# Two channel tiles per scan with start states from TensorE in layer 0, and separate banks and later steps for the token chain in layers 1 and 2

## The reference, cut to what matters

```python
# layer 0: selective scan over the 2304 pixels of an image, 768 inner channels, 16 states
xz = xs @ in_proj_w.T                 # 384 -> 1536: xin and gate z
xin = silu(causal_conv4(xin) + conv_b)
dt, Bm, Cm = split(xin @ x_proj_w.T);  dt = softplus(dt @ dt_proj_w.T + dt_proj_b)
h = exp(dt * A) * h + dt * Bm * xin   # per pixel, channel and state
y = einsum(h, Cm) + xin * D;           out = layernorm((y * silu(z)) @ out_proj_w.T)
# layer 1: 1x1 product, a filter on 8x8 blocks in the Fourier domain, 3x3 depthwise, gelu gate, 1x1 product
# layer 2: 11x11 depthwise convolution whose kernels have 4 free points
# layer 3: two of four experts per pixel, each 384 -> 384 -> 384
```

## Time and profile before

| | us |
|---|---|
| three runs | 6280.98 median, 6262.24 to 6282.42 |
| profiled execution | 6270.08, of which span 6268.3 |
| TensorE busy | 5086.3 (81%) |
| DVE busy | 4781.1 (76%) |
| ACT busy | 2805.0 (45%) |
| POOL busy | 2379.9 (38%) |
| mean granted TensorE clock | 0.927 |

### The profile page before, as it was taken

The page is one execution under the profiler, slowest core; times in us unless marked ns, Lnnn a source line. Parts: engine busy times, 40 slices in busy tenths (PEclk is TensorE's granted clock), DMA queues, the critical chain, the costliest instruction groups (busy, mean ns, idle before and its releaser), DMA issues.

```text
span 6268.3 us, 78225 instructions
## 1 busy us (share of the span) xinstructions
PE 5086.3 (81%) x28644; PEld 3933.0 (63%) x28644; DVE 4781.1 (76%) x6523; ACT 2805.0 (45%) x4858; POOL 2379.9 (38%) x2894
## 2 busy tenths in 40 slices
PE   5787888887888887888888876677777787999999
PEld 3565656655656655666655554355555576999998
DVE  3999999999999999999999997637373753333333
ACT  3555555555555555555555552213131322333332
POOL 3544455544455544545554443334243430000000
PEclk8999999999999999999999998788888898999999
DMA  1000000000000000000000001000101010000000
GB/s 67 1 16 23 8 8 8 8 16 23 8 8 8 8 16 23 8 8 8 8 8 8 8 5 37 0 32 12 35 12 35 12 54 26 31 31 23 31 31 20
DMA packets 73548, 115.49 MB, mean 18 GB/s; under 512 B 4132, under 2 KB 70208, under 8 KB 73164
## 3 DMA queue, kind: packets, MB, share of 16 engines
q1 hardware_dynamic: 73164, 110.48, 5.3%
HBM read 68.00 MB, written 42.47 MB: 18 GB/s over the span
## 4 chain that ended last, share of the span: by engine, by line
PE 44%; DVE 28%; issue 16%; ACT 8%; POOL 3%; DMA 0%; SPq 0%; DVEq 0%; ACTq 0%; POOLq 0%
DVE a_h L720 13%; PE pw L1606 7%; DVE a_acc L734 7%; PE ps L1573 6%; PE pw L436 5%; PE ps L347 4%; PE ps L428 3%; PE ps L971 2%; PE ps L387 2%; ACT a_dA L561 2%; PE pw L1573 2%; POOL b_xw L1450 2%; PE ps L1059 2%; PE pw L1059 2%; PE ps L1015 1%
## 5 line engine op out<-in xcount | busy, mean ns | idle before, releaser
L720 DVE TENSOR_TENSOR_SCAN a_h<-a_dA,a_st,ps 128x384 f32<-128x384 f32 x1920 | 1861.8, 997 | 77.1 <-PE ps L428 74.3
L561 ACT ACTIVATE a_dA<-a_dt,a_Aneg 128x384 f32<-128x384 f32 x2304 | 1320.2, 607 | 481.8 <-DVE a_h L720 475.6
L824 POOL TENSOR_SCALAR a_dBT<-a_dtxT,a_BC 128x768 f32<-128x768 f32 x1152 | 1057.8, 936 | 818.9 <-PE ps L428 817.8
L428 PEld LDWEIGHTS ps<-g_ident,a_dBT 128*128 128x128 f32 x6912 | 885.5, 146 | 734.8 <-DVE a_h L720 328.4
L428 PE MATMUL ps<-g_ident,a_dBT 128*128 128x128 f32 x6912 | 1191.4, 285 | 181.3 <-DVE a_h L720 171.5
L436 PE MATMUL pw<-g_ident,a_h 128*128 128x128 f32 x6912 | 1023.0, 289 | 122.6 <-DVE a_h L720 120.6
L734 DVE SCALAR_TENSOR_TENSOR a_acc<-pw,a_BC,a_acc 128x768 f32<-128x768 f32 x1080 | 1070.4, 991 | 33.1 <-PE pw L436 32.3
L436 PEld LDWEIGHTS pw<-g_ident,a_h 128*128 128x128 f32 x6912 | 835.7, 149 | 188.2 <-DVE a_h L720 179.7
L1714 DVE TENSOR_TENSOR d_hf<-d_hf,ps 128x384 f32<-128x384 f32 x288 | 159.1, 554 | 560.3 <-ACT d_hf L1644 553.0
L387 PE MATMUL ps<-a_xn,a_WinT 128*128 128x384 f32 x864 | 380.8, 527 | 91.9 <-DVE a_dt L625 41.5
L327 PE MATMUL ps<-a_WoT,a_sz 128*128 128x384 f32 x864 | 362.8, 504 | 73.7 <-ACT a_ob L448 68.1
(11 more groups left out here) (232 smaller groups left out, 9131.9 us busy)
## 6 DMA issues: line engine op xcount, KB each, us to landing
a_xs<-in_x SPq DMA_DIRECT2D x24, 576.0 KB, 3.9
x<-a_xs SPq DMA_DIRECT2D x24, 576.0 KB, 3.0
b_x<-x SPq DMA_DIRECT2D x24, 576.0 KB, 4.4
e_xs<-x SPq DMA_DIRECT2D x24, 576.0 KB, 3.8
out<-e_xs SPq DMA_DIRECT2D x24, 576.0 KB, 3.0
a_sx<-in_x SPq DMA_DIRECT2D x19, 576.0 KB, 3.9
x<-b_x SPq DMA_DIRECT2D x16, 576.0 KB, 3.1
x<-b_x SPq DMA_DIRECT2D x4, 936.0 KB, 3.7
```

The lines of the kernel that those rows point to most:

```text
L428: t = e.transpose(m[f"ps{idx % 3}"][:, tb * 128:(tb + 1) * 128], m[f"a_dBT{g % 2}"][:, tb, c * 128:(c + 1) * 128], ident[:])
L561: e.activation(m[f"a_dA{idx % NDA}"][:], m[f"a_dt{k % 2}"][:, c, :], ACT.Exp, scale=m["a_Aneg"][:, c, n:n + 1]).then_inc(s["a_exp"], 1)
L720: e.tensor_tensor_scan(m[f"a_h{g % 2}"][:, c, :], m[f"a_dA{idx % NDA}"][:], m[f"ps{idx % 3}"][:, 0:T], 0.0 if q == 0 else m["a_st"][:, c, ...
L824: t = e.tensor_scalar(m[f"a_dBT{g % 2}"][:, tb, :], m[f"a_dtxT{o}"][:, tb, :], m[f"a_BC{o}"][:, tb, n:n + 1], 1.0, ALU.mult, ALU.mult)
```

## The change

**Layer 0.** A scan takes two channel tiles: `a_dA`, `a_h` and the PSUM buffer have 385 columns per tile instead of 384, of which the first is a start column. There `a_dA` is zero, so the scan sets itself to the value that stands in the PSUM buffer's start column, and the scan's own start is the constant 0. That value comes from TensorE: a product of the identity with two columns of `a_st` (or of zeros in an image's first chunk). The buffers are `pw0` and `pw1`, two banks each; the transposes of `h` have a single buffer, `pw2`, and lag three pairs instead of following the state's end. `a_acc` is there twice, so nothing stands after a chunk's steps. `a_dA` has 5 pairs instead of 12 tiles. TensorE takes side work only before every second step (`every=2`), and its side work has two banks, `ps3` for readers on ACT (`S`) and `ps2` for readers on DVE (`D`). The convolution of all six tiles is on POOL and ACT. The transposes of `a_acc` stand at steps 7 to 14 instead of 0 to 8. Statistics are loaded a channel tile at a time.

**Layers 1 and 2.** The first product goes to `pw2`, the Fourier product to `pw0`, the inverse product alternates between two banks and ACT copies every token. The places of the mixing part are new and no longer scaled by 0.9. A unit's sparse products stand before its patches, patches 2 and 3 go together, and POOL weighs a row's three channel tiles in three units instead of one. The output product alternates between two banks instead of three.

```diff
-LEAD = 8
-NDA = 12
+PAIRS = STEPS // 2
+COL = 511 - (T + 1)
+LEAD = 7
+NDA = 5
-POOL_CONV = (0, 2, 3, 5)
-DVE_CONV = (1, 4)
-A_AT = (0, 2, 3, 5, 6, 8)
+A_AT = (7, 8, 10, 11, 13, 14)
...
     for n in range(steps):
-        due(n)
+        if n % every == 0:
+            due(n)
...
+    def inputs(k, p):
+        pi, q = PAIRS * k + p, k % NQ
+        g, c = NS * k + p // 3, 2 * (p % 3)
+        ps = m[f"pw{pi % 2}"]
+        w.wait_ge("p_dbt", g + 1)
+        w.wait_ge("v_scan", pi - 1)
...
+        first = m["a_st"][:, c:c + 2, p // 3] if q > 0 else m["a_zero"][:]
+        for h in range(2):
+            for tb in range(TB):
+                at = COL + h * (T + 1) + 1 + tb * 128
+                e.transpose(ps[:, at:at + 128], m[f"a_dBT{g % 2}"][:, tb, (c + h) * 128:(c + h + 1) * 128], ident[:])
+        e.matmul(ps[:, COL:COL + T + 2:T + 1], ident[:], first, start=True, stop=True, skip_group_check=True).then_inc(s["pe_b"], 1)
+    def turned(hh):
+        g, tb = divmod(hh, TB)
+        w.wait_ge("v_scan", 3 * g + 3)
+        w.wait_ge("v_acc", hh)
+        for c in range(6):
+            t = e.transpose(m["pw2"][:, c * 128:(c + 1) * 128], m[f"a_h{g % 2}"][:, c, 1 + tb * 128:1 + (tb + 1) * 128], ident[:])
...
         def main(n):
...
+            if n % 2 == 0:
+                inputs(k, n // 2)
+            elif PAIRS * k + n // 2 >= TB:
+                turned(PAIRS * k + n // 2 - TB)
-        march(side, STEPS + 3, main)
+        march(side, STEPS, main, every=2)
...
+    def scan(k, p):
...
+        e.tensor_tensor_scan(m[f"a_h{g % 2}"][:, c:c + 2, :].rearrange("p c t -> p (c t)"), m[f"a_dA{pi % NDA}"][:].rearrange("p c t -> p (c t)"),
+                             m[f"pw{pi % 2}"][:, COL:COL + 2 * (T + 1)], 0.0, ALU.mult, ALU.add).then_inc(s["v_scan"], 1)
...
-    for u, i in enumerate(POOL_CONV):
+    for i in range(6):
         yield 12 + 3 * i
...
-PACE = UNITS / 60
...
 def win_at(n):
-    return 12.5 + 0.7 * n
+    return 11.5 + 0.75 * n
 def conv_at(g, k):
-    return 20 + 10.5 * g + 1.1 * k
+    return 20 + 8.6 * g + 0.95 * k
...
+def mix_banks(m):
+    return m["ps0"], m["pw0"][:, 0:512], [m["pw0"][:, 512:1024], m["pw1"][:, 0:512]]
...
-            TF.claim("a_tT", NT * b + n + 1)
+            w.wait_ge("a_tT", NT * b + n)
...
-    return [] if bi + 1 == BLOCKS else [4 * bi + 4 + i for i in ((0, 1), (2,), (3,))[c]]
+    return [] if bi + 1 == BLOCKS else [4 * bi + 4 + i for i in ((0, 1), (2, 3), ())[c]]
...
-    if u % 9 == 6 and u // 9 + 2 < NQ:
-        pixels_pool(e, m, w, b, u // 9 + 2)
+    q, i = divmod(u, 9)
+    if i >= 6 and q + 2 < NQ:
+        pixels_pool(e, m, w, b, q + 2, i - 6)
```

389 lines of the change are left out of this document (184 added, 205 removed).

## The result

| | us |
|---|---|
| kernel before, 4 runs | 6281.1 median, 6262.2 to 6282.4 |
| changed kernel, 4 runs | 6177.0 median, 6174.5 to 6233.6 |
| ratio | 0.987, 95% interval 0.985 to 0.990 |
| profiled execution | 6176.2 (before 6270.1) |
| mean granted TensorE clock | 0.944 (before 0.927) |

What follows compares the result with a forecast made beforehand. DVE and TensorE were taken to bound layer 0 within a few per cent of each other. From 6270 us, minus 139 (layer 0), plus 8 (first chunk's convolution), minus 42 (layers 1 and 2) gave 6097, so 6100; range 5880 to 6260.

Steps and rivals of the forecast that it cites:

- times 24: Layer 0: a chunk of 150.5 us against 156.3, taken for all 24 chunks, minus 139 us.
- The rival in which TensorE stays hidden: Layer 0: hand-overs, POOL's lag and ACT's Silus hide as before; total 5909 us, chance 0.25.
- The rival of the single buffer for the turned states: Layer 0: transposes of h wait for the accumulation before; chunk 154.3 us, total 6190, chance 0.13.
- Merged scans: Layer 0, DVE: one scan of two tiles takes 1.64 us, a beat 2.55; minus 8.1 us a chunk.
- Convolution: Layer 0: moving it off DVE saves 5.0 us a chunk; POOL's lag adds 2.5, bounded by 0 and 7.
- The state matmul: Layer 0, TensorE: a 128x2 product writing each pair's start values, 0.22 us each, 10.6 us a chunk.
- Full pairs: Layer 0: pairs with two side matmuls take TensorE 2.82 us, over DVE's 2.55; plus 5.1 us a chunk.
- Hand-overs and accumulator transposes: Layer 0: side-bank users with nothing between, plus 3.9 us a chunk; accumulator transposes through DVE's bank, plus 1.4.
- Silus before the output product: Layer 0: the output product's wait for ACT now falls into TensorE-bound pairs; plus 2.5 us a chunk (0.5 to 5).
- Solo tokens: First batch alone, before layer 2: a token takes 3.3 us instead of 4.35, saving 19 us in all.
- Woven batches: Three batches beside layer 2: at most 38 us of token-chain waits saved, against plus 15 (0 to 60) for other edits.
- The lower clock: Rival: TensorE's lower-clock stretches fall on TensorE-bound pairs of layer 0; chunk 159.9 us, total 6322, chance 0.12.

Runs made afterwards that it cites:

- every_step: Changed kernel with TensorE's side work of layer 0 before every step instead of every second: 6074.2 us, ratio 0.971.
- both_back: Changed kernel with the order in a unit, spread weighing and all places of layers 1 and 2 undone, only their banks kept: 6157 us, ratio 0.985.
- l0_only: Layer 0 of the changed kernel with layers 1 and 2 of the kernel before: 6170.0 us, ratio 0.987.
- order_back: Changed kernel with only the order in a unit undone, patches before sparse products on TensorE and DVE: 6166 us, ratio 0.981.
- filler: Changed kernel with 32 unread 128x128 products before the first output product of each image third in the woven batches: 6175.8 us, ratio 0.984.

## Why the prediction was wrong, and where it was right

**The steps that failed.** The forecast summed to 173 us and the profiled executions differ by 94. The larger miss, 50 us, is the sum for the woven batches: minus 38 for the waits of the token chain taken at full value, plus 15 for all other edits in one lump, and nothing for TensorE's clock, which had a price in layer 0 only. The runs show about minus 4 for the banks (not clear of the scatter) and plus 45 for the order in a unit; and TensorE is busy 26 us longer for the same work, nearly all of the 28 us by which the batches grew. The smaller miss, 34 us, is the mean chunk of layer 0 "times 24". That the time still lies in the range of 5880 to 6260 says little, since this range took in most of the rivals.

**Two bounds in layer 0: right in kind.** DVE waits almost only for TensorE's inputs, with 11.6 us of idle time in a typical chunk where the forecast had 14. The forecast's 150.5 us was a mean, though, and it meets the typical chunk (150.2) partly by luck: the mean of the 22 inner chunks is 152.7, with 139.9 of DVE's work and 12.9 of idle time. The rival in which TensorE stays hidden (idle time stays at 6.8, a chunk of 143.3) is out. The rival of the single buffer for the turned states priced it at 154.3 us; the wait is there (410 us of TensorE's idle time before L438), and no run removed it, so its share is open.

**Term by term.** *Merged scans*, -8.1: the beat is 2.58, not 2.55, so -7.7 in a chunk that starts from states and only -1.4 in the one of six that starts from zero, -6.7 in the mean. *Convolution*, -5.0 + 2.5: DVE's part was 5.0 (8 instructions in a chunk, start to start); GpSimd's lag shows as 1.1 us behind step 16 and 1.8 behind step 22, less the 0.26 that neighbours show, 2.4. Undoing it cost 3.8 a chunk. *The state matmul*, 0.22: 0.14 from its start to the next one's between transposes, but leaving it out shortens a full pair by 0.18 and a second one lengthens it by 0.22. *Full pairs*, 2.82: 2.78. *Hand-overs and accumulator transposes*, 3.9 + 1.4: `every_step` gave 3.1 in a typical chunk and 4.1 in the mean. *Silus before the output product*, 2.5: the profile's page puts 24.0 us of TensorE's waiting on it in all (L329 waiting for ACT `a_ob`), 1.0 a chunk.

**What failed in layer 0** (34 us, against -131) is the step "Times 24" with its mean, and a cost that was not seen:
- The two chunks at the ends have no neighbour's side work. They went from 137.0 to 137.9 and from 136.1 to 133.0, not down by 5.8 each: 9 us.
- The 22 others went from 157.2 to 152.7, by 4.4 instead of 5.8: 31 us. DVE's work in them fell by 10.3 us instead of 13.1 (the merged scans are 1.4 of the difference, the rest is not located), and its idle time grew by 5.8 instead of 7.2. In that idle time are 14 us of waiting for the statistics' loads (L672 above), and some 15 us are five chunks of 153 where 150.2 is usual, three of which have a granted clock of 0.98 instead of 1.00.
- The first chunk's convolution cost 2.7 us, not 8: 5 us the other way.

**Solo tokens: right**, 3.25 us against 3.3. The stage gained 26.5 us instead of 19, but banks alone gave 13, the new places some of the rest, and the same code takes 200 to 208 us from one execution to the next; this one was at the short end.

**Woven batches: wrong in every term.** The step was "in the three woven batches at most the 38 us of the earlier trace rows", with "I price these together at plus 15 (0 to 60)". The 38 us of waits did go, and brought some 4 us (`both_back` against `l0_only`): by the estimate above the batches would be 28 us shorter at the full clock, and more time at the lower clock takes 24 back. Taking such waits at full value was the mistake; "at most" was then used as the value itself. And the order in a unit, named in the forecast but priced in one lump, costs 45 us (`order_back`). The waits show its way: DVE's addition waits 247 us instead of 59 for a product that was just issued, and holds up what stands behind it.

**The lower clock.** The rival had the mechanism and the wrong place. It was argued for layer 0, where the clock rose. Over the woven batches it fell from 0.87 to 0.81, and TensorE was busy 758 us instead of 732 for the same work and with the same idle time. That this is cause and not company rests on `filler` in its stage and on the same code at three clocks; in the total it could not be shown. The estimate puts all of the order's 45 us down to the clock. It comes from one execution of each kernel, and the order and the clock were not changed separately, so this split is not shown by an experiment. Why the new order leaves TensorE at the lower level for longer, with nearly the same idle time in all (189 and 199 us), is open too.

## What to carry to other kernels

A wait that the profile shows inside a loop of several engines is worth its length only if nothing else in the loop is nearly as late; look at the second wait on the same engine before summing the first. Price every edit of an order by itself, by what it puts in front of what on the queue that others wait for. Look at the granted clock of every stage whose waits a change moves, also where the sum of the waits stays the same. When two engines bound a stage within a few per cent, where the side work stands (every step or every second) can be worth as much as the work that the change removes.

## What the runs showed of the hardware

- A scan that starts from a value in SBUF costs 0.06 us more than one that starts from a constant (2.74 against 2.61 us for a beat of two); merging two scans of 385 into one of 770 saves 0.04 us in all.
- DVE's 64x768 product takes 0.95 us alone, 1.61 beside a GpSimd instruction that reads one tensor from SBUF and 2.58 beside its addition of two; DVE's 128x768 convolution steps take 1.00 to 2.63. The reverse holds too: GpSimd's additions of 768 in layer 1 take 1.80 to 2.52 us, and those of 384 in layer 0 fell from 1.06 us to 1.00 when DVE's convolution left, where the forecast estimated 0.05.
- A 128x2 fp32 product: the next instruction starts 0.14 us after its start between transposes. Where TensorE sets the pace, leaving it out saves 0.18 us a pair and a second one costs 0.22.
- The same three batches of work took 950 to 980 us as the time at TensorE's lower clock went from 363 to 423 us, with the same idle time.
- More work for TensorE can shorten a stage: 10.5 us of useless products in each batch raised the granted clock over the three from 0.81 to 0.85, and they took 939 us.
